# A two-block transformer kernel: the first three modulation pieces as TensorE products, half projections spread over the first scores, GpSimd's work reordered

## The reference, cut to what matters

```python
mod = (_silu(L0_c) @ L0_wmod).reshape(1, 6, 1, -1)      # c: 1x512, wmod: 512x3072
sa, ca, ga, sb, cb, gb = (mod[:, 0], ..., mod[:, 5])
h = _layernorm(x) * (1 + ca) + sa
x = x + ga * attention(h, Wq, Wk, Wv, Wo)               # 32 query heads, 8 key heads, width 16, rotary, causal
h = _layernorm(x) * (1 + cb) + sb
x = x + gb * moe_ffn(h)
mod = (_silu(L1_c) @ L1_wmod).reshape(1, 6, 1, -1)      # the second block: a state-space mixer,
...                                                     # then a gated feed-forward with low-rank parts
```

## Time and profile before

| | us |
|---|---|
| median of 3 runs | 810.98 |
| lowest and highest | 810.4, 812.01 |
| the profiled execution's own time | 809.74 |
| its span | 807.7 |
| TensorE busy in it | 732.0 (91%) |
| VectorE, ScalarE, GpSimd busy | 480.2, 323.1, 337.8 |
| mean granted TensorE clock | 0.968 of full speed |

### The profile page before, as it was taken

The page is one execution under the profiler, slowest core; times in us unless marked ns, Lnnn a source line. Parts: engine busy times, 40 slices in busy tenths (PEclk is TensorE's granted clock), DMA queues, the critical chain, the costliest instruction groups (busy, mean ns, idle before and its releaser), DMA issues.

```text
span 807.7 us, 10131 instructions
## 1 busy us (share of the span) xinstructions
PE 732.0 (91%) x3654; PEld 440.6 (55%) x3654; DVE 480.2 (59%) x715; ACT 323.1 (40%) x536; POOL 337.8 (42%) x277
## 2 busy tenths in 40 slices
PE   4897999889999999879999999799778999997998
PEld 2443333333343332148678888454447788875886
DVE  3758777677778776246565457767785333336311
ACT  3311266566766766751245311454243333222100
POOL 0227993785475553671165332213532222124300
PEclk9998899999999999999999999999789999998999
DMA  9442624150550500230033200213000110111111
GB/s 312 151 116 68 141 79 90 68 115 15 102 108 10 115 3 2 95 99 7 0 83 100 65 1 1 72 43 65 34 6 27 53 52 26 52 52 52 40 66 39
DMA packets 24110, 52.99 MB, mean 66 GB/s; under 512 B 4252, under 2 KB 8100, under 8 KB 23044
## 3 DMA queue, kind: packets, MB, share of 16 engines
q1 hardware_dynamic: 24068, 52.44, 23.7%
HBM read 45.63 MB, written 6.60 MB: 65 GB/s over the span
## 4 chain that ended last, share of the span: by engine, by line
PE 68%; DVE 12%; issue 8%; POOL 6%; ACT 3%; DMA 1%; SPq 1%; ACTq 0%; DVEq 0%; POOLq 0%
PE ps L862 65%; DVE mxp L1755 3%; PE ps L879 2%; ACT pr L1411 1%; DMA rq<-in_mask 1%; POOL wsum L2165 1%; DVE st L1597 1%; POOL pr L2181 1%; POOL x L2275 1%; DVE xnb L1621 1%; DVE x L1943 1%; DVE arena L1640 1%; PE ps L1028 1%; POOL wmr L2163 1%; POOL rs L2094 1%
## 5 line engine op out<-in xcount | busy, mean ns | idle before, releaser
L862 PE MATMUL ps<-arena 128*128 128x512 f32 (+1 forms) x1416 | 332.1, 395 | 7.9 <-DVE arena L1640 4.2
L862 PEld LDWEIGHTS ps<-arena 128*128 128x128 f32 (+1 forms) x1416 | 264.8, 188 | 68.2 <-DVE arena L1640 6.1
L1755 DVE TENSOR_REDUCE mxp<-ps 128x2 f32<-128x1024 f32 (+3 forms) x160 | 172.6, 1114 | 55.0 <-PE ps L862 53.3
L1411 ACT ACTIVATE pr<-ps 128x512 f32<-128x512 f32 x288 | 162.3, 596 | 86.5 <-PE ps L862 84.0
L862 PE MATMUL ps<-Qst,Kst 99*128 99x512 bf16 x288 | 103.0, 388 | 9.5 <-ACT pr L1411 7.4
L862 PE MATMUL ps<-Kst,Qst 96*128 96x512 bf16 (+3 forms) x384 | 101.5, 336 | 7.6 <-DVE mxp L1755 5.8
L2181 POOL TENSOR_TENSOR pr<-pr,cap 128x512 int32<-128x512 int32 x56 | 70.7, 1278 | 32.8 <-ACT pr L1411 32.6
L862 PE MATMUL ps<-pr,vr 128*32 128x512 f32 x576 | 76.8, 606 | 5.0 <-POOL pr L2181 4.3
L862 PEld LDWEIGHTS ps<-Kst,Qst 96*128 96x128 bf16 x384 | 35.8, 99 | 66.3 <-DVE mxp L1755 26.8
L862 PEld LDWEIGHTS ps<-Qst,Kst 99*128 99x128 bf16 x288 | 26.6, 98 | 82.3 <-ACT pr L1411 60.9
L2280 POOL TENSOR_TENSOR arena<-raw,arena 128x1024 fp32r<-128x1024 f32 x11 | 27.1, 2467 | 84.3 <-ACT arena L1477 84.3
(11 more groups left out here) (197 smaller groups left out, 821.2 us busy)
## 6 DMA issues: line engine op xcount, KB each, us to landing
wmr<-in_wmr SPq DMA_DIRECT2D x8, 1280.0 KB, 11.3
raw<-in_w SPq DMA_DIRECT2D x16, 512.0 KB, 3.3
Qst<-q_parts SPq DMA_DIRECT2D x42, 128.0 KB
q_parts<-qparts SPq DMA_DIRECT2D x3, 768.0 KB, 3.7
x<-in_x SPq DMA_DIRECT2D x8, 256.0 KB, 6.4
wm<-in_wm SPq DMA_DIRECT2D x4, 512.0 KB, 7.4
raw<-in_up SPq DMA_DIRECT2D x8, 256.0 KB, 2.6
raw<-in_down SPq DMA_DIRECT2D x8, 256.0 KB, 2.6
```

The lines of the kernel that those rows point to most:

```text
L862: return nc.tensor.matmul(outp, lhs, rhs, start=start, stop=stop, skip_group_check=True)
L1411: A(pr[:, k % PRING, :], ps[:, 4 + k % 2, :], ACT.Exp, scale=float(DH) ** -0.5).then_inc(exp_done, 1)
L1755: V.tensor_reduce(mxp[:, kh, g0:g0 + heads, i].rearrange("p (b e) -> p b e", e=per), units, AXX, ALU.max)\
```

## The change

- **Modulation.** `MOD_BY_PE = 3`: pieces 0, 1 and 2 are no longer weighed by GpSimd. `mod_step(h)` for h < 3 multiplies the raw weights in `wmr` by the conditioning columns in 16 matmuls of 160 columns. GpSimd keeps pieces 3 to 7, and `head_pool(n)` now ends with `weigh(n + 1)`, in place of `weigh(n + 2)`. SyncE loads the next piece after storing the last row for h < 3, and after `wsum_ready` for later ones.
- **Half projections.** The same ten halves, in another order, behind units 0, 1, 2, 4, 6, 8, 10, 13, 16, 19. The four halves of `queries(3, ..)` now stand ahead of units 0 to 3 of head 1. `values(0)` stands ahead of `ln_turn(0, 1)`, and `ln_turn(0, 0)` is interleaved with mod0.
- **GpSimd and VectorE.** Both `sines` of a half come ahead of `key_lo`; `rope_queries(2)` waits for the first `mparts`; `swap_queries(1)` and `(2)` move to unit 6 of head 0 and unit 2 of head 1.

```diff
-FILL = (("v", 1), ("q", 1, 0), ("q", 1, 1), ("q", 2, 0), ("q", 2, 1))
+FILL = (("q", 1, 0), ("q", 1, 1), ("v", 1), ("q", 2, 0), ("q", 2, 1))
+FILL_HALVES = [(job, range(2 * h, 2 * h + 2)) for job in FILL for h in range(2)]
+FILL_AT = (0, 1, 2, 4, 6, 8, 10, 13, 16, 19)
+MOD_BY_PE = 3
...
             def head_dmas(h):
-                if h < NKV - 1:
-                    sp.wait_ge(wsum_ready, h + 1)
-                    sp.dma_start(wmr[:, :, :].rearrange("p c n -> p (c n)"), a["wmr"][h + 1]).then_inc(wmr_in, 16)
+                if MOD_BY_PE <= h < NKV - 1:
+                    sp.wait_ge(wsum_ready, h - MOD_BY_PE + 1)
+                    load_mod(h + 1)
                 sp.wait_ge(mt_parts, h + 1)
...
+                if h < MOD_BY_PE:
+                    load_mod(h + 1)
...
             keys(0)
             pe.wait_ge(wq_sorted, KC)
             queries(0, 0)
+            values(0)
             ln_turn(0, 1)
             keys(1)
             queries(0, 1)
-            values(0)
...
             def mod_step(h):
                 pe.wait_ge(s_read, slots_before(h, NS + 1) - 1)
-                pe.wait_ge(wsum_ready, h + 1)
                 w = MODW // 4
+                if h < MOD_BY_PE:
+                    pe.wait_ge(wmr_in, 16 * h + 16)
+                    for kc in range(KC):
+                        for q in range(4):
+                            last = mm(ps[32 * q:32 * q + 32, 2, 0:w], sc32[:, kc, :, :].rearrange("p l m -> p (l m)"),
+                                      wmr[:, kc, w * q:w * q + w], kc == 0, kc == KC - 1)
+                    last.then_inc(s_full, 1)
+                    return
+                pe.wait_ge(wsum_ready, h - MOD_BY_PE + 1)
...
             max_turn(0)
-            queries(3, 0)
             mod_step(0)
             pe.wait_ge(st_in[1], 144)
             for s in range(AHEAD):
+                if s < 4:
+                    queries(3, s // 2, range(2 * (s % 2), 2 * (s % 2) + 2))
                 s_unit(1, s)
-                if s in (1, 3):
-                    queries(3, 1, range(s - 1, s + 1))
...
                 sines(2 * hf)
+                sines(2 * hf + 1)
                 key_lo(hf)
-                sines(2 * hf + 1)
...
             def head_pool(n):
                 head_v(n)
-                work = weighing(2) if n == POOL_MASKED else iter(())
                 for r in range(ROUNDS):
                     mask_round(n, r)
-                    if r > 0:
-                        next(work, None)
-                for _ in work:
-                    pass
-                if n + 2 < NKV:
-                    weigh(n + 2)
+                if MOD_BY_PE <= n + 1 < NKV:
+                    weigh(n + 1)
...
             head_v(0)
-            weigh(0)
+            pool.wait_ge(mt_parts, 1)
             rope_queries(2)
-            weigh(1)
             rope_queries(3)
```

More of the change, by code:

```diff
@@ L725, in _, with load_mod @@
                 sp.dma_start(sinb[:, tok[hf]], a["sin"][:, tok[hf]]).then_inc(trig_in[hf], 16)
-            sp.dma_start(wmr[:, :, :].rearrange("p c n -> p (c n)"), a["wmr"][0]).then_inc(wmr_in, 16)
+            def load_mod(h):
+                sp.dma_start(wmr[:, :, :].rearrange("p c n -> p (c n)"), a["wmr"][h]).then_inc(wmr_in, 16)
             def load_keys(n, tok_, done):
@@ L871, in hilo, with ln_turn @@
                 return f(pair[0]), f(pair[1])
-            def ln_turn(L, hf):
+            def ln_turn(L, hf, chunks=range(KC)):
                 pe.wait_ge(ln_xn, 8 * L + 4 * hf + 4)
-                for c in range(KC):
+                for c in chunks:
                     b = bank_of(pe, ("ln", L, hf, c))
@@ L904, in _ @@
             for kc in range(KC):
+                if kc == KC - 1:
+                    pe.wait_ge(ident_in, 16)
+                    ln_turn(0, 0, (0,))
                 pe.wait_ge(wm0_in[kc], 16)
@@ L1062, in _ @@
                 s_unit(0, s)
[L1063 to L1069, removed]
+                for at, (job, half) in zip(FILL_AT, FILL_HALVES):
+                    if at == s:
+                        if job[0] == "v":
+                            values(job[1], half)
+                        else:
+                            queries(*job[1:], half)
                 if s == VT_AT:
@@ L1383, in _ @@
             values_out(0)
+            for hf in range(2):
+                queries_out(1, hf)
             values_out(1)
-            for c in (1, 2):
-                for hf in range(2):
-                    queries_out(c, hf)
             for hf in range(2):
@@ L1391, in _ @@
                     .then_inc(read_b[b], 1)
-            for hf in range(2):
-                queries_out(3, hf)
+            for c in (2, 3):
+                for hf in range(2):
+                    queries_out(c, hf)
             def copy_ctx(n):
@@ L1807, in _ @@
                 s_unit(0, s)
[L1808 to L1809 removed]
+                if s == 6:
+                    swap_queries(1)
             evacuated(dve, ("vT", 1))
@@ L1813, in _ @@
                 s_unit(1, s)
+                if s == AHEAD // 2 - 1:
+                    swap_queries(2)
             swap_queries(3)
@@ L2147, in head_v, with weigh @@
                 nc.gpsimd.tensor_copy(vr[:, :, 0:DH], vtok[:, :, n * DH:(n + 1) * DH]).then_inc(vr_ready, 1)
-            def weighing(h):
+            def weigh(h):
                 pool.wait_ge(wmr_in, 16 * h + 16)
-                if h:
+                if h > MOD_BY_PE:
                     pool.wait_ge(s_full, slots_before(h - 1, NS + 1) + 1)
```

18 lines of the change are left out of this document (9 added, 9 removed).

## The result

The change makes the kernel slower. The changed kernel took 832.12 us in the median of four runs (827.46 to 833.09), the kernel before, on the same chip, 811.5 us (810.4 to 813.55). The ratio is 1.0243, with a 95% interval of 1.0207 to 1.0279. The profiled execution of the changed kernel took 833.09 us, with a span of 831.3; that of before took 809.74 and 807.7.

A forecast was written before the change was run, and what follows sets the result against it. TensorE was taken as the bound, with about one microsecond of slack in a head body. From 809.74 us, net gains of 11.2 came off, waits added 22.4 and lower clock 8.0: 828.9, said as 829; range 815 to 838.

The forecast's parts named there:

- (a): Heads 2 to 6: TensorE waits five times for `wsum`, 6.7, three of 4.4, and 2.9 us; 22.4 us taken in all.
- Rival 2: The weighing is ready before TensorE asks, so no waits and 798.5 us; chance 0.12.
- (b): Behind the five waits TensorE's granted clock falls to 0.5 for some 3 us each; 8.0 us in all.
- rival 1: The five waits come but the low clock does not, or seldom: 821 us; chance 0.26.
- (c): Head 1 takes 33 us with no wait for a mask; heads 1 and 2 gain 4.0 and 2.5 us.
- (d): In the start, the first transposed unit comes near 86 us; a gain of 7.4 us.
- The poorer end: Start gains only 5.5 us: TensorE idles 2.5 us before the loaded `Kst`, which may bring a low clock stretch.
- Head 0: GpSimd no longer weighs piece 1 beside VectorE's splitting of the maxima; the wait for `full` goes, gaining 1.5 us.
- (e): Mod steps 0 to 2, made by TensorE, take 1.9 us each, 1.4 us more each.
- (f): After the mod steps, TensorE does not wait for the small `mparts` transfers with the maxima's rows.
- Rival 3: The maxima's rows come late behind the next piece's load; TensorE waits some 3 us in four heads, 841; chance 0.10.
- Rival 4: The change does little in the start, 3 us less gained: 832 us; shares the forecast's chance of 0.52.

The follow-up runs named there:

- the dealt one: Changed kernel with weighings one head earlier, low-rank products ahead of piece 3, and piece 3 spread before `vr` and among head 2's masks: 798.79 us, ratio 0.9813.
- the filled run: Changed kernel with 28, 19, 19, 19 and 12 needless products ahead of the `wsum` waits in mod steps 3 to 7: 819.78 us, ratio 1.0091.
- the start part: Kernel before with only the half projections, `values(0)`, sines and query order changed; GpSimd weighs all eight pieces as before: 815.46 us, ratio 1.0042.
- the modulation part alone: Kernel before with pieces 0 to 2 by TensorE and 3 to 7 weighed at the end of the head needing them, old start: 838.03 us, ratio 1.0296.
- the run with half of each wait filled: Changed kernel with 20, 10, 10, 4 and 4 needless products ahead of the five `wsum` waits: 828.4 us (two runs), ratio 1.0190.
- the run with early weighing: Changed kernel with GpSimd weighing piece n + 2 at the end of `head_pool(n)`, as the kernel before does: 811.68 us, ratio 0.9982.

## Why the prediction was right

The forecast was 829, the measurement 832.12; sign, place and mechanism were as said. That it came so near is in part luck, since misses of both signs went into the sum (the last paragraph adds them up). By its own points:

**(a) The waits.** 22.2 us for a forecast of 22.4. The five are 6.49, 4.32, 4.32, 4.32 and 2.77, said to be 6.7, three of 4.4, and 2.9. GpSimd goes from mask to weighing without a gap, and a weighing took 8.46 us (213.91 to 222.37), where the earlier trace rows had 8.60. Rival 2 (ready in time) is out; the kernel that makes it true, the dealt one, took 798.79, and 798.5 was its price. That the two are so near is chance: its profile has a rest 3.4 us longer than before, a start 5.0 us shorter, head 0 1.5 and heads 1 to 3 together 5.7 us shorter, and these are not the terms of 798.5.

**(b) The clock.** It fell behind all five, so rival 1 (821) is out. The term was too small: 8.0 for what the filled run shows to be 12.0. Its step "in a stretch where TensorE is the bound, 3.2 us at half clock cost 1.6" took the length of the low stretch from one wait of 1.82 us. To halve the length was right where TensorE is the bound, but the lengths differ: behind the first four waits the work at the lower clock lasted 5.6, 4.6, 4.0 and 3.8 us (to 189.6, 227.1, 264.6 and 302.2 us) and cost 2.7, 2.2, 1.9 and 1.8. Behind the last, of 2.77 us, it lasted about 10 us (from 336.3 to 346.6) and cost 3.5:

```profile
336.00:338.00 2.00, 1.71 (x10) 0.58 0.00 0
...
344.00:346.00 2.00, 2.00 (x10) 0.50 1.01 238
346.00:348.00 2.00, 2.00 (x11) 0.86 0.85 303
```

The ends I gave for this term, 0 and 8.0, did not hold it: "all of the five" was not the upper end, since one can cost more than 1.6.

**(c) Heads 1 and 2.** Head 1 came to 32.42 us, forecast 33, with no wait for a mask. The gain of both, 6.5, can be read off the filled run: heads 1 and 2 take 70.53 us there and took 69.83 before; less 6.5 for the wait and 0.8 for the mod step, that is a gain of 6.6.

**(d) The start.** The first transposed unit came at 87.27, forecast "near 86". Without mod step 0 the gain is 6.2 (5.4 + 0.8) for 7.4. The poorer end (5.5) was named for the right reason, the idle ahead of the scores, but that was 4.63 us and not 2.5, and the profiles with `values(0)` moved back put the lower clock behind it at 1.6 to 1.7 us in this kernel. The part that was not seen at all is that this gain hangs on the modulation part. Alone the start part is a loss of 0.42%.

**Head 0.** 1.5 less, with mod step 1 in it, so 2.3 without, for 1.5. The wait of 1.47 us for `full` is gone, but the prediction named the wrong neighbour. In the kernel before, GpSimd had weighed piece 1 by 107 us; what lay beside VectorE's splitting was the rotary work of chunk 3. One of VectorE's four instructions was held by it, as in the side by side above:

```profile
118.72 2.25 DVE L1769 TENSOR_TENSOR mt<-mt,mparts 32x128 f32<-32x128 f32 x1
118.69 2.13 POOL L2138 TENSOR_TENSOR qparts<-qacc,qparts 128x1024 bf16<-128x1024 f32 x1
```

In the changed kernel the rotary work ends at 111.31 us, ahead of the splitting, but it lies beside the instruction that makes `nm` (1.94 us for 1.12 before), and TensorE waits 1.20 us for that. With the modulation part alone TensorE has neither of these waits, and head 0 takes 36.71 us.

**(e) The mod steps.** 1.29 us for 1.9; as what a head is longer by, 0.8 for 1.4. The step "four groups of 0.48 us in place of one" was too dear: 32 records took 1.29 us, 2.7 times what eight take and not four times. The two ends, 1.4 and 2.3, both lay too high. (The 0.8 is measured in heads 3 to 5 of the kernel with all pieces by TensorE; that it holds for steps 0 to 2 is taken over from there.)

**(f) `mparts`.** No wait for them. In the stretch behind the mod step of head 3 they landed in 5.2 us, close to the 5.3 of the earlier trace rows:

```profile
Qst<-mparts SPq DMA_DIRECT2D x3, 8.0 KB, 5.2
```

Rival 3 is out. Nor did the small ones come in behind the whole load there: it landed at 229.10 us, and they at 228.02, 228.60 and 229.56. Rival 4 (little from the start, 832) named the number, and the two things it feared, a wait for `Qst` and a new low stretch, did come; but the start gave 1.2 less than forecast, not 3, so it is right in its number by luck.

Set against the 4.1 us by which the profiled execution exceeds the forecast (833.09 and 829), the misses are: clock +4.0, start +1.2, mod steps -1.8, head 0 -0.8, waits -0.2, heads 1 and 2 -0.1, and +2.2 in the rest, which no edit touches. That is 7.4 too much and 2.9 too little, together 4.5. They are differences of spans, and by the spans the miss is 4.4 (23.6 for a forecast of 19.2), so next to nothing stays open.

## What to carry to other kernels

Ask of every product at what moment it is asked for and what the engine that makes it has queued ahead of that: one head earlier was worth up to 34 us here (22.2 of waits and 12.0 of lower clock; the dealt kernel was 33 shorter), while the work itself was cheap on either engine. A wait of the bounding engine has a second price, the half clock behind it, which here was about half as large as the waits themselves; take it from a stretch with a wait of the same length, and do not take the dearest case seen for an upper end. Two parts of a change that share an engine have to be tried apart and together, since one may pay only where the other has made room.

## What the runs showed of the chip

**TensorE's clock after short idles.** With 1.80, 2.04, 2.06 and 2.06 us of idle in one execution the clock fell to 0.50 behind three and stayed at 1.00 behind one, that of 2.04. A still shorter wait, 1.33 to 1.38 us for VectorE's maxima shortly behind the first transposed unit, stands in the profiles of all twelve kernels: the lower clock came with it in four (0.50 in the window of 98 to 100 us in the kernel before, behind 1.35 us) and not in the other eight. The kernel with the start part alone adds a case: the wait of 2.45 us of the earlier trace rows had no low clock behind it, and its counterpart of 2.48 us had.

```profile
176.38 1.94 PE L865 MATMUL ps<-pr,vr 128*32 128x512 f32 x8 [2.48 <-POOL pr L2189]
```

```profile
178.00:180.00 2.00, 2.00 (x9) 0.50 0.85 265
```

The five waits of the changed kernel (2.77 to 6.49 us), the one of 3.35 us in the run with half of each wait filled, the one of 10.71 us in the run with early weighing, and the idle of 3.81 to 4.67 us ahead of the first scores all had it. But a length of this size is no safe sign either: in the kernel before, TensorE idles for 3.00 us up to 508.38 us, behind the attention, and the clock is 1.00 in all windows from 502 to 512 us.

**VectorE beside GpSimd.** A VectorE instruction of 0.21 to 0.28 us (32 partitions, 128 elements) took 1.16 to 2.12 us beside GpSimd's instructions of 1024 columns (1.05 to 2.35 us), and ended 0.08 to 0.14 us behind them. The copy out of PSUM that follows them (L1779, 0.30 us) was not longer beside GpSimd than without it. I had counted GpSimd's overlap with VectorE as nearly free, since neither was the bound; four such instructions on the way to the maxima made TensorE wait for 4.46 us.
